# First attention of a two-layer adaLN kernel: the inversion of the softmax sums on ScalarE and the product with it on VectorE, each two units later

## The reference, cut to what matters

```python
xn = _ln(x, g_attn, b_attn)
qkv = (xn @ qkv_w + qkv_b).reshape(b, s, 3, H, HD)        # H = 16, HD = 8
scores = jnp.einsum('bhqd,bhkd->bhqk', q, k) / np.sqrt(HD)
scores = jnp.where(causal[None, None], -jnp.inf, scores)
attn_w = jax.nn.softmax(scores, axis=-1)
attn = jnp.einsum('bhqk,bhkd->bhqd', attn_w, v)
attn = attn.reshape(b, s, d) @ out_w + out_b
```

## Time and profile before

| what | value |
|---|---|
| median of three runs | 1017.04 us (1012.84 to 1019.17) |
| the profiled execution | 1007.75 us, of which the span from first to last instruction is 1006.0 us |
| granted TensorE clock, mean over the span | 0.978 |
| PE busy | 932.9 us (93%) |
| DVE busy | 621.9 us (62%) |
| ACT busy | 554.8 us (55%) |
| POOL busy | 460.2 us (46%) |
| first attention | from about 40 us to about 304 us of the span |

### The profile page before, as it was taken

The page is one execution under the profiler, slowest core; times in us unless marked ns, Lnnn a source line. Parts: engine busy times, 40 slices in busy tenths (PEclk is TensorE's granted clock), DMA queues, the critical chain, the costliest instruction groups (busy, mean ns, idle before and its releaser), DMA issues.

```text
span 1006.0 us, 21539 instructions
## 1 busy us (share of the span) xinstructions
PE 932.9 (93%) x7391; PEld 600.5 (60%) x7391; DVE 621.9 (62%) x2056; ACT 554.8 (55%) x1075; POOL 460.2 (46%) x697
## 2 busy tenths in 40 slices
PE   8999999999989989999996798889997999999997
PEld 3566777777654223334642796456664644499995
DVE  4788888888824975872553454578772653344444
ACT  5536676766666554574521474567875622255551
POOL 1146777777741955640056464344552043323331
PEclk9999999999999997999999899999997999999999
DMA  6720000000001000031011335000000000121115
GB/s 216 240 72 13 8 13 13 10 10 13 13 20 76 0 0 1 0 121 47 1 35 45 82 96 192 13 2 1 3 1 1 1 30 29 34 61 49 50 30 178
DMA packets 38329, 45.82 MB, mean 46 GB/s; under 512 B 7840, under 2 KB 31648, under 8 KB 37360
## 3 DMA queue, kind: packets, MB, share of 16 engines
q1 hardware_dynamic: 33712, 35.13, 11.6%
q0 software_dynamic: 4512, 9.32, 2.8%
HBM read 31.19 MB, written 18.69 MB: 50 GB/s over the span
## 4 chain that ended last, share of the span: by engine, by line
PE 81%; ACT 6%; DVE 6%; issue 3%; POOL 2%; DMA 1%; SPq 0%; DVEq 0%; ACTq 0%; POOLq 0%
PE PS L686 5%; PE PS L703 5%; PE PS L693 5%; PE PS L444 5%; PE PS L486 5%; PE PS L340 4%; PE PS L637 4%; PE PS L639 4%; PE PS L646 4%; PE PS L457 4%; PE PS L349 3%; PE PS L546 2%; PE PS L437 2%; PE PS L813 2%; PE PS L794 2%
## 5 line engine op out<-in xcount | busy, mean ns | idle before, releaser
L922 ACT ACTIVATE pw<-PS 128x384 f32<-128x384 f32 x256 | 111.6, 488 | 71.2 <-PE PS L466 68.5
L1602 POOL TENSOR_SCALAR_AFFINE_SELECT pw<-pw 128x256 f32<-128x256 f32 x256 | 104.6, 432 | 75.3 <-ACT pw L922 73.1
L1200 DVE CUSTOM_DVE_ANT_0 PS<-PS,above 128x256 f32<-128x256 f32 x256 | 115.9, 453 | 31.4 <-PE PS L437 31.2
L1668 POOL DMA_INDIRECT token_rows<-xnb,slot_in x77 | 73.8, 958 | 104.3 <-ACT xnb L1028 104.3
L1654 POOL TENSOR_TENSOR XS<-XS,N 128x512 f32<-128x512 f32 x64 | 81.1, 1289 | 57.1 <-DVE N L1278 34.6
L444 PE MATMUL PS<-kf,qm 32*128 32x256 f32 x512 | 103.4, 426 | 0.5 <-POOL qm L1611 0.5
L1454 DVE TENSOR_TENSOR rsb<-sqb,PS 128x256 f32<-128x256 f32 (+1 forms) x77 | 42.6, 553 | 84.6 <-PE PS L693 84.0
L1202 DVE CUSTOM_DVE_ANT_0 PS<-PS,above 128x128 f32<-128x128 f32 x256 | 84.6, 330 | 0.0
L1624 POOL TENSOR_SCALAR_AFFINE_SELECT pw<-pw 128x256 f32<-128x256 f32 x128 | 55.9, 471 | 59.8 <-ACT pw L1073 59.8
L1611 POOL TENSOR_SCALAR qm<-qs,qmask 128x256 f32<-128x256 f32 x64 | 59.5, 931 | 44.7 <-ACT kf L903 44.7
L1011 ACT ACTIVATE sqb<-PS 128x512 f32<-128x512 f32 x48 | 28.7, 597 | 89.2 <-PE PS L637 89.2
(11 more groups left out here) (214 smaller groups left out, 2363.4 us busy)
## 6 DMA issues: line engine op xcount, KB each, us to landing
sorted_rows<-empty_rows_dram SPq DMA_DIRECT2D x2, 2535.0 KB, 14.7
slot_in<-sorted_rows SPq DMA_DIRECT2D x77, 65.0 KB, 1.9
N<-token_rows SPq DMA_DIRECT2D x16, 256.0 KB, 4.6
X<-xT_dram SPq DMA_DIRECT2D x8, 256.0 KB, 5.6
token_rows<-empty_rows_dram SPq DMA_DIRECT2D x1, 2048.0 KB, 24.9
ATT<-gate_dram SPq DMA_DIRECT2D x1, 2048.0 KB
XS<-down_dram SPq DMA_DIRECT2D x1, 2048.0 KB
H<-up_dram SPq DMA_DIRECT2D x1, 2048.0 KB
```

The lines of the kernel that those rows point to most:

```text
L922: nc.scalar.activation(pw[:, w % 2, j + n, :], PS[:, A_PST + (2 * v + n) % 3, 0:3 * P], ACT.Exp).then_inc(a_p, 1)
L1200: nc.vector.tensor_tensor_reduce(x[:, 0:SEQ], x[:, 0:SEQ], above[:, :], 1.0, -3e38, ALU.add, ALU.max, mx[:, t // 8 % 2, 1, j, g:g + 1])
L1602: m = nc.gpsimd.affine_select(x[:, :, SEQ * k:SEQ * k + P], x[:, :, SEQ * k:SEQ * k + P], [[0, 2], [1, P]], ALU.is_ge, 0.0, base=0, channe ...
L1668: nc.gpsimd.indirect_dma_start(token_rows[l][:, :], bass.IndirectOffsetOnAxis(slot_in[:, r, D:D + 1].bitcast(mybir.dt.int32), 0), slot_out ...
```

## The change

`invert_sums` of batch b moves from unit 8(b + 3), u = 0, to 8(b + 3) + 2, u = 2, for the first 14 batches. `normalise` moves from 8(b + 3) + 2, u = 2, to u = 4 for the first 13 batches and to u = 3 for batch 13 (which is projected in that same unit). Batches 14 and 15 keep their places, and so do `out_project`, `add_bias`, `keep_weighed` and the DMAs. No instruction is added or removed.

```diff
-        NORM_STEPS = {8 * (b + 3) + 2 if b < BATCH - 2 else 8 * (b + 2) + 6: b for b in range(BATCH)}
+        NORM_STEPS = {8 * (b + 3) + (4 if b < BATCH - 3 else 3) if b < BATCH - 2 else 8 * (b + 2) + 6: b for b in range(BATCH)}
...
-        INVERT_STEPS = {8 * (b + 3) if b < BATCH - 2 else 8 * (b + 2) + 5: b for b in range(BATCH)}
+        INVERT_STEPS = {8 * (b + 3) + 2 if b < BATCH - 2 else 8 * (b + 2) + 5: b for b in range(BATCH)}
```

## The result

The changed kernel takes 1032.27 us (median of four runs, 1031.35 to 1037.41), beside 1017.72 us for the kernel before. The ratio over all runs is 1.016, with a 95% interval of 1.013 to 1.019 (the two medians alone give 1.014). So it is slower by over 1%, where 1025.0 us and "within 1%, on the slow side" was forecast, and it lies just outside the range. The profiled execution took 1031.35 us, with a span of 1029.6 us.

What follows compares the result with a forecast made beforehand. The prediction took PE to pace the attention loop. It summed 7.0 us for thirteen batches and 1.0 us for the loop's end to 8.0 us, added to the median of 1017.04 us: 1025.0 us, range 1018 to 1032 us.

Steps and rivals of the forecast that it cites:

- Away from u = 0: nothing: Logarithm and exponential leaving ACT between the exponentials of u = 0 and u = 1: gain taken as 0.
- Rival 2: The gap at u = 1 is ACT's after all: 0.50 us a batch comes back, 1018.5 us; 12%.
- Exponentials of u = 3 late by 0.25 us: Inversion on ACT in u = 2 delays the next exponentials, and PE's start of u = 4, by 0.25 us.
- A gain of 0.17 us from the product's old place, used up: Product leaving DVE at u = 2 returns 0.17 us of PE's wait for maxima, net 0.08 us late at u = 4.
- The copy's wait, 0.54 us a batch: At u = 4 ACT's copy L929 waits for DVE's product, delaying later exponentials and PE's u = 6: 0.54 us a batch.
- Rival 3: The copy's wait is covered, the product being over by the copy's start: 2.0 us remain, 1019 us; 10%.
- The lock: DVE's product overlapping POOL's cuts at u = 4: POOL pays 0.45 us, covered; DVE 0.08, product kept at 0.77 us.
- Rival 1: The product at u = 4 lets both POOL cuts pass, copy another 0.50 us late: 14.5 us, 1031.5 us; 15%.
- Thirteen batches, 7.0 us: In the loop, batches 0 to 12 each cost 0.54 us at PE's u = 6: 7.0 us in all.
- The end of the loop: 1.0 us: Batch 13's projection in unit 131 waits for its product, and all units behind it follow 1.0 us later.

Runs made afterwards that it cites:

- tail_only: The change for batch 13 alone, batches 0 to 12 as in the kernel before: 1026.81 us against 1018.59, ratio 1.0072.
- copies_alone: Kernel before with only the product of batches 0 to 12 moved to u = 4, and two buffers for the copy of the sums: 1015.94 us against 1018.22, ratio 0.9974.
- product_u3: Kernel before with, for batches 0 to 12, logarithms at u = 2 and the product at u = 3: 1021.76 us against 1017.16, ratio 1.0046.
- loop_only: The change for batches 0 to 12, batch 13 as in the kernel before: 1025.52 us against 1018.59, ratio 1.007.
- tail_filled: The whole change plus one spare PE matmul of 512 columns ahead of batch 13's projection: 1027.17 us against 1018.59 for the kernel before, ratio 1.0086.
- both_mended: The whole change plus two buffers for the copy of the sums and one spare matmul ahead of batch 13's projection: 1018.86 us against 1016.57 before, ratio 1.0017.
- copies_masks: copies_alone plus POOL's two masks for the next batch at u = 5 and 6 instead of 6 and 7: 1014.32 us against 1018.22 before, ratio 0.9969.
- two_copies: loop_only plus two buffers for the copy of the sums: 1019.07 us against 1018.59 for the kernel before, ratio 1.0003.

## Why the prediction was right, and where it was wrong

- **Away from u = 0: nothing.** Right. From u = 0 to u = 2 PE takes 179.71 - 175.88 = 3.83 us, and its gap ahead of u = 2 is 0.46 us, as before (at 163.30). Rival 2 is out. This holds for the usual batch. In a short one (see the last section) this stretch takes 3.46 us in the kernel after and 3.63 in tail_only and copies_alone, where the logarithms stand at u = 0: there the move is worth 0.17 us.
- **Exponentials of u = 3 late by 0.25 us.** Right: 1.96 us between the pairs (180.77 to 182.73) where 1.95 were summed, and 0.22 or 0.23 us a batch in each of three comparisons.
- **A gain of 0.17 us from the product's old place, used up.** Right. It appears as 0.18 us when the copy's wait is taken away (copies_alone). In the kernel after, the stretch between the weighings (L486) of u = 2 and u = 4 is 0.06 us longer and that from u = 4 to u = 6 0.48 us, where 0.08 and 0.46 were forecast.
- **The copy's wait, 0.54 us a batch.** Right step by step. The first maximum comes 0.96 us after PE's unit, the product 1.23 us after that, the copy 0.86 us after the product (0.80 were summed), PE's u = 6 1.12 us after the copy (1.17). From u = 2 to u = 6 PE takes 7.81 us against 7.27, which is 0.54. Rival 3 is out.
- **The lock.** Right: the product still takes 0.77 us and starts 0.19 us into the cuts, which take 1.22 us. Both moved to u = 4 together. Rival 1 is out, although its time, 1031.5 us, is nearly the one measured: a right number from a wrong mechanism. The Trainium skill ("SBUF — State Buffer", "Who interferes with whom") has the instruction issued second wait for the whole of the first. Taken one by one, the second cut goes that way: issued 0.17 us behind the product, it takes 0.86 us instead of 0.41. The product, issued 0.19 us into the first cut, pays only 0.08 us, and nothing in product_u3, where it starts 0.05 us ahead of the cuts and takes 0.69 us.
- **Thirteen batches, 7.0 us.** A little too much: 4.93 us in the profiled execution up to batch 12, since five of twelve batches took 15.00 and not 15.37 us. In loop_only, where nearly all are long, it is 6.5 us. The short batches come from the cast of the last section, which the prediction didn't have: that the loop came out cheaper was luck.
- **The end of the loop: 1.0 us. This is the step that failed.** The wait is there, 1.35 us long, and delays the projection by 1.18 us; the mechanism was right. But the sum let all units behind it "follow" at their old durations. PE's clock fell behind the wait, and at 1.2 GHz these units took another 8.46 us: 9.6 us for a term put at 1.0. tail_only shows this term by itself. In tail_filled and both_mended, with the wait filled, the clock stays up behind it and batch 14 follows after the old 7.21 us.
- **The range.** It reached to 1032 us for another reason (rival 1), with no case in it for the clock. The earlier trace rows show that this kernel's clock does fall elsewhere, and I used them only to say that the change doesn't touch that. The Trainium skill ("TensorE: Matmul & The Clock Gate", "HAM oscillation — how this bites in real kernels") warns that idle gaps of PE can throttle it; the gaps it names are longer than the 1.35 us here, so the row goes further than the page.

## What to carry to other kernels

A wait on the bounding engine is priced twice: what it takes, and what the clock does behind it; where a trace has stretches at half clock at all, give a new wait of a microsecond or more a case of its own, with the work behind it at the other level. A step that is moved later is cheap only if its buffer is free of the next write: look for who overwrites its inputs, and double that buffer first (here 0.47 us a batch). And look at what stands right behind the new place on its engine, since one unit earlier or later was worth up to 0.50 us a batch (u = 3 against u = 4 with two buffers), nearly as much as the whole move in the loop (0.52).

## What the runs showed of the hardware that was not expected

**The clock at the end stands on an edge.** PE at 1.00 fell to 0.50 within 2 us behind a wait of 1.35 us, and stayed there for some 24 us, though PE was 90 to 100% busy in the stretches shown of them. Judging by time and mean clock this befell twelve of the fourteen executions with that wait unfilled (the kernel after and tail_only). But the length of one wait does not decide it alone: in the kernel after, a wait of 1.48 us that ended at 278.97 us was followed by clock 1.00, and so it was in the three other profiles that have it. And copies_masks lost the clock in a wait of 1.03 us, which stands in the kernel before in the same units, with the same wait of 0.60 us ahead of it, and cost it nothing; it cost four of thirteen profiles the clock. What tells these cases apart is not settled here. With the wait of 1.35 us filled, the clock held behind it in both profiles. For the wait of 1.03 us there is one filled profile, which proves little beside nine unfilled ones that kept the clock.

**A cast of 128 x 32 takes 0.24 or 0.50 us.** In the kernel after, the cast L1211 and the subtraction L1213 in the timeline of DVE, in a short batch and in the long one behind it:

```profile
161.23 0.24 DVE L1211 CAST mxs<-mx 128x32 bf16<-128x32 f32 x1
161.50 0.29 DVE L1213 TENSOR_TENSOR mxr<-mx,mxs 128x32 f32<-128x32 f32 x1
...
176.22 0.50 DVE L1211 CAST mxs<-mx 128x32 bf16<-128x32 f32 x1
176.76 0.40 DVE L1213 TENSOR_TENSOR mxr<-mx,mxs 128x32 f32<-128x32 f32 x1
```

and POOL's cuts beside them:

```profile
160.87 0.86 POOL L1602 TENSOR_SCALAR_AFFINE_SELECT pw<-pw 128x256 f32<-128x256 f32 x2
...
175.86 0.77 POOL L1602 TENSOR_SCALAR_AFFINE_SELECT pw<-pw 128x256 f32<-128x256 f32 x2
```

Where DVE is quick the cuts take 0.09 us longer, which looks like the same lock with the other one paying; no run here shows that by itself. It is far cheaper if POOL pays: cast and subtraction are 0.26 + 0.11 = 0.37 us shorter, and so is such a batch, since the maxima lead straight to PE's u = 2 (3.46 us from its u = 0 instead of 3.83). With the logarithms at u = 0 only 0.20 us of it arrive (3.63 us in tail_only and copies_alone). The cast starts 0.36 us into the cuts in both, so what flips it cannot be seen in these rows. It fell the short way in five of twelve batches of the kernel after, in three of twelve of two_copies (14.51 us), in two of tail_only, whose loop is that of before, and in none of the kernel before's (0.49 us at the least in the loop). So it isn't the change that brings it about.
